# Two attention layers and a mixture of experts on one core: the program rewritten so that two heads share the array in 64-row tiles

## What is computed

```python
def attn_a(x):                       # 16 heads of 16 features
    q, k, v = x @ Wq.T + bq, x @ Wk.T + bk, x @ Wv.T + bv
    scores = q @ k.T / 4 - slope[h] * |pos_q - pos_k|     # -inf where pos_k > pos_q
    return softmax(scores) @ v @ Wo.T + bo
def attn_b(x):                       # K, Q, V = split(x @ W_KQV.T); rope on Q and K; causal
    return softmax(rope(Q) @ rope(K).T / 4) @ V @ W_O.T
def ffn(x):                          # 8 experts, two per token, chosen by expert_indices
    ys = gelu(xs @ w1[e]) @ w2[e]    # xs: token rows sorted by expert
    return sum over the two of ys * weight, for 1024 tokens, + bias
x = x + attn_a(layernorm(x)); x = x + ffn(layernorm(x))
x = x + attn_b(layernorm(x)); x = x + ffn(layernorm(x))
```

## Time and profile before

| what | value |
|---|---|
| median of three runs | 5482.74 us (5477.25 to 5489.55) |
| the profiled execution, first to last instruction | 5479.5 us |
| TensorE busy | 4942.7 us, 90% |
| VectorE busy | 3575.6 us, 65% |
| ScalarE busy | 3156.7 us, 58% |
| GpSimd busy | 584.8 us, 11% |
| granted TensorE clock, mean | 0.956 |

### The profile page before, as it was taken

One profiled execution on the slowest core, in us unless ns is written; L12 is line 12 of the kernel. 1 busy time (PEld: TensorE's weight loads), 2 busy tenths in 40 slices (PEclk: granted clock), 3 DMA queues, 4 the chain that ended last, 5 costly groups with the idle time before them and its releaser, 6 DMA issues.

```text
span 5479.5 us, 115362 instructions
## 1 busy us (share of the span) xinstructions
PE 4942.7 (90%) x29820; PEld 2236.2 (41%) x29820; DVE 3575.6 (65%) x9222; ACT 3156.7 (58%) x6661; POOL 584.8 (11%) x1479
## 2 busy tenths in 40 slices
PE   5999899998999899969689998999979998899897
PEld 2333433343333433358433334333433334333376
DVE  5778577857776677730377765778567785777600
ACT  2777566765666466732246772667536674566622
POOL 1000110011000200020210002000110002100101
PEclk9999999999999999989899998999989999999998
DMA  4221121103110311045221101211021111111154
GB/s 110 48 35 22 44 58 35 29 25 71 31 32 8 80 28 35 15 144 182 75 49 25 31 8 41 57 30 25 25 56 29 25 19 42 42 31 25 53 169 142
DMA packets 193432, 278.45 MB, mean 51 GB/s; under 512 B 45000, under 2 KB 155848, under 8 KB 192224
## 3 DMA queue, kind: packets, MB, share of 16 engines
q1 hardware_dynamic: 189664, 261.84, 20.4%
q0 software_dynamic: 3072, 8.39, 0.5%
HBM read 124.59 MB, written 43.25 MB: 31 GB/s over the span
## 4 chain that ended last, share of the span: by engine, by line
PE 73%; issue 11%; DVE 6%; ACT 5%; POOL 2%; DMA 1%; SPq 1%; ACTq 1%; DVEq 0%; another core or an unknown queue 0%; POOLq 0%
PE ps_acc L824 18%; PE ps_s L796 17%; PE ps_m L771 15%; ACT probs L597 3%; PE ps_s L931 3%; PE ps_s L748 3%; PE ps_o L834 3%; PE ps_s L799 2%; PE ps_m L941 2%; PE ps_o L941 2%; PE ps_s L910 2%; DVE ps_m L1048 2%; ACT acc_sb L590 2%; PE ps_acc L748 1%; DVE parts L1119 1%
## 5 line engine op out<-in xcount | busy, mean ns | idle before, releaser
L597 ACT ACTIVATE probs<-ps_s 128x512 f32<-128x512 f32 (+3 forms) x5120 | 2459.2, 538 | 1110.1 <-PE ps_s L796 641.7
L1051 DVE TENSOR_REDUCE part_max<-ps_m 128x1 f32<-128x512 f32 x3072 | 1998.2, 684 | 318.1 <-PE ps_m L771 317.1
L771 PE MATMUL ps_m<-stacks 108*128 108x512 bf16 (+7 forms) x5120 | 1790.0, 354 | 156.7 <-DVE part_max L1051 69.6
L796 PE MATMUL ps_s<-stacks 111*128 111x512 bf16 (+7 forms) x5120 | 1757.3, 356 | 98.5 <-issue 54.6
L1048 DVE CUSTOM_DVE_ANT_0 ps_m<-ps_m,mask 128x128 f32<-128x128 f32 (+3 forms) x2048 | 1002.8, 500 | 491.4 <-PE ps_m L771 482.0
L824 PE MATMUL ps_acc<-probs,v_head 128*32 128x512 f32 (+3 forms) x11264 | 1272.1, 516 | 1.9
L796 PEld LDWEIGHTS ps_s<-stacks 111*128 111x128 bf16 (+1 forms) x5120 | 498.7, 98 | 1362.9 <-ACT probs L597 997.1
L771 PEld LDWEIGHTS ps_m<-stacks 108*128 108x128 bf16 (+1 forms) x5120 | 503.3, 98 | 702.1 <-DVE part_max L1048 229.3
L799 PE MATMUL ps_s<-early,identb 128*128 128x128 bf16 x2048 | 453.7, 222 | 0.0
L824 PEld LDWEIGHTS ps_acc<-probs,v_head 128*32 128x32 f32 x11264 | 315.2, 108 | 333.1 <-issue 145.2
L504 POOL CAST cpart<-negmax 128x8 bf16<-128x8 f32 x256 | 50.8, 198 | 3315.2 <-DVE negmax L1056 3315.2
(11 more groups left out here) (114 smaller groups left out, 3362.7 us busy)
## 6 DMA issues: line engine op xcount, KB each, us to landing
stacks<-parts SPq DMA_DIRECT2D x1536, 64.0 KB
stacks<-w_dram SPq DMA_DIRECT2D x60, 1024.0 KB
stacks<-crow SPq DMA_DIRECT2D x768, 2.0 KB
xn<-x_in_dram SPq DMA_DIRECT2D x4, 2048.0 KB, 15.8
xb<-x_in_dram SPq DMA_DIRECT2D x4, 2048.0 KB, 8.4
x_before_ffn<-xb SPq DMA_DIRECT2D x8, 1024.0 KB, 5.2
x_after_a<-parts SPq DMA_DIRECT2D x4, 2048.0 KB, 10.7
xn<-x_after_a SPq DMA_DIRECT2D x4, 2048.0 KB, 15.0
```

Source lines behind the costliest of these rows:

```text
L597: act.activation(probs[:, n % 8, 0:QW - q0], ps_s[:, s_bank(j, n)[0], q0:QW], ACT.Exp)\
L771: pe.matmul(ps_m[:, bank, 0:w], q_stack(slot)[0:rows, qb * P:(qb + 1) * P], k_stack(slot)[0:rows, kc * QW:kc * QW + w], start=True, stop=T ...
L796: mm = pe.matmul(ps_s[:, bank, q0:QW], k_stack(slot)[0:rows, kb * P:(kb + 1) * P], q_stack(slot)[0:rows, qt * QW + q0:(qt + 1) * QW], star ...
L1051: dve.reduce_max(part_max[:, qb, kc:kc + 1], ps_m[:, bank, 0:w], AX_X).then_inc(item_used, 1)
```

## The change

The whole program is written anew. What it computes, the ffn's tiles and the order of layers and batches are the same. What differs:

- **Two heads at once.** A pair of heads has one q and one k stack, one head in rows 0 to 63 and the other in rows 64 to 127: 48 product rows (three products of two parts), 4 rows of positions, 2 of the maximum. The stacks are of type float32r instead of bf16. Scores (`score`, L817) and maxima (`unit`, L842) are issued as matmuls of 54 or 52 rows for head 0 and head 1 in turn, into different banks.
- **36 steps for 40 blocks.** On the diagonal the block 384 wide and the one 128 wide share a bank (`STEP`, `UNIT`), so that one exponential serves both. All masks are added by TensorE, 64 columns at a time (L825, L850), for the maxima too.
- **Maxima.** VectorE takes the maxima of both heads in one instruction over two banks (L1074), from two pairs of banks `ps_p`. It splits the maximum itself, in two parts.
- **Values.** Groups of two or three steps; the four 32-column tiles are now head 0 and 1 x outer and inner query blocks, 256 columns each (L874). They sum up in `ps_acc` by themselves: `sum_up` and `turn_sum` are gone. ScalarE copies 256 columns (L718) and SP stores them to DRAM in four transfers (`store_o`, L541).
- **Banks.** Scores of both heads and the five kinds of TensorE's job (`RING_JOBS`) take turns in one ring of three banks, `ps_r`.
- **Fronts and backs inside the heads.** `batch_jobs` cuts the next batch's front and the last batch's back into jobs (`ld`, `ln`, `xt`, `qk`, `v`, `sp`, `st`; `rl`, `bl`, `bm`, `y`, `ba`, `bs`) of one quarter batch or less, and hangs them on steps of the pairs. Those of TensorE stand two by two behind the values at seven of the 18 double steps (`JOB_STEPS`). The norm of 512 rows is cut in eight parts (`norm`), with Newton steps from an integer estimate instead of a square root on ScalarE. Q and k parts go to DRAM (`parts_d`) and come back per pair; rope swaps neighbours by transfer (`sw`) instead of by a second projection.
- **No loops.** All 64 pairs are written out. The first batch's front stands alone ahead of them, the last batch's back among the last ffn's tiles (`AFTER_AT`). The first ffn stops the pairs at the half; its gather and sum run within the next pair.

The core of the diff:

```diff
-BLOCK = [(qt, kb, max(0, P * (kb - 4 * qt))) for qt in reversed(range(NQ)) for kb in range(4 * qt + 4)]
...
+STEP = [slot for qt in reversed(range(NQ)) for slot in
+        [[(qt, kb, 0, 0)] for kb in range(4 * qt + 1)] +
+        [[(qt, 4 * qt + 1, P, 0), (qt, 4 * qt + 3, 3 * P, 3 * P)], [(qt, 4 * qt + 2, 2 * P, 0)]]]
...
+        while at:
+            n = 3 if len(at) == 3 else 2
+            groups.append(at[:n])
+            at = at[n:]
...
+JOB_STEPS = (2, 10, 16, 20, 24, 28, 34)
...
+            def score(g, n, heads):
...
+                for at, (qt, kb, q0, col) in enumerate(STEP[n]):
+                    for u in heads:
+                        if at == 0:
+                            pe.wait_ge(ring_used, PLACE[("s", g, n, u)] - RING + 1)
+                        r = slice(HALF * u, HALF * u + ROWS)
+                        mm[u] = pe.matmul(block_bank(g, n, u)[:, col:col + QW - q0], ks[s][r, kb * P:(kb + 1) * P],
+                                          qs[s][r, qt * QW + q0:(qt + 1) * QW], start=at == 0, stop=True,
+                                          skip_group_check=True)
+                for qt, kb, q0, col in STEP[n]:
+                    for part in range(2 if kb >= 4 * qt else 0):
+                        for u in heads:
+                            r = slice(HALF * u, HALF * u + HALF)
+                            lo = col + HALF * part
+                            mm[u] = pe.matmul(block_bank(g, n, u)[:, lo:lo + HALF], mk[r, 2 + part, :], id64[r, :],
+                                              start=False, stop=True, skip_group_check=True)
...
+            def unit(g, n):
...
+                if at >= 2:
+                    pe.wait_ge(p1_used, at - 1)
...
+            def times_v(g, grp):
...
+                        for u in range(2):
+                            for inner in range(2):
+                                chunks = [c for c in ((1, 2) if inner else (0, 3)) if c >= first]
...
+                                mm = pe.matmul(ps_acc[tile:tile + DH + 1, to[0] * P:(to[-1] + 1) * P],
+                                               v_head[:, beta % 2, kb, 2 * p + u, :], src, start=kb == 0,
+                                               stop=n == GROUP[LAST_GROUP[qt]][-1], skip_group_check=True)
...
-                pieces = [(r, r, BLOCK[4 * g + r][2], QW) for r in range(4)]
...
-            def sum_up(ly, hb, h):
...
+            def exp_block(g, n, u):
+                w, at = step_width(n), STEPS * g + n
+                if at >= PBUF:
+                    act.wait_ge(pv_mm, groups_to(at - PBUF))
+                act.wait_ge(s_mm[u], at + 1)
...
+                for qb, kc, w, col in UNIT[n]:
+                    mm = dve.tensor_reduce(part_max[:, :, qb, kc], ps_p[:, p1_banks(g, n), col:col + w], AX_X, ALU.max)
+                mm.then_inc(p1_used, 1)
```

More of the change, by code:

```diff
@@ new lines, with value_groups @@
+assert STEPS == len(UNIT) == 36
+HI_UNITS = sum(1 for slot in UNIT if slot[0][0] >= TT // 2)
+FIRST_LO = next(n for n, slot in enumerate(STEP) if slot[0][0] == 1)
+def value_groups():
+    groups = []
+    for qt in reversed(range(NQ)):
+        at = [n for n, slot in enumerate(STEP) if slot[0][0] == qt]
+        while at:
+            n = 3 if len(at) == 3 else 2
+            groups.append(at[:n])
+            at = at[n:]
+    return groups
+GROUP = value_groups()
+GROUPS = len(GROUP)
+GROUP_OF = {n: i for i, steps in enumerate(GROUP) for n in steps}
@@ new lines, with slots_from @@
+GROUP_AT = {2 * (steps[-1] // 2 + 1): i for i, steps in enumerate(GROUP)}
+assert len(GROUP_AT) == GROUPS and GROUP_AT[STEPS] == GROUPS - 1
+LAST_GROUP = {qt: max(i for i, steps in enumerate(GROUP) if STEP[steps[0]][0][0] == qt) for qt in range(NQ)}
+EVAC_STEP = {qt: 2 * (GROUP[i][-1] // 2 + 1) + 1 for qt, i in LAST_GROUP.items() if qt}
+LATE_EVAC = 1
+C_HI, C_LO = 30, 6
+JOB_STEPS = (2, 10, 16, 20, 24, 28, 34)
+assert all(n in GROUP_AT for n in JOB_STEPS + (C_HI, C_LO))
+def slots_from(t, n):
+    found = []
+    while len(found) < n:
+        if t % STEPS in JOB_STEPS:
+            found += [t, t]
+        t += 1
+    return found[:n]
@@ new lines, in store_o @@
+            def store_o(g, qt):
+                e = evac_index(g, qt)
+                beta, p = divmod(g, PAIRS)
+                sp.wait_ge(acc_out, e + 1)
+                for u in range(2):
+                    row = o_d[beta % 2, 2 * p + u, :, qt * QW:(qt + 1) * QW].rearrange("r (c n) -> r c n", n=P)
+                    for inner in range(2):
+                        to = row[:, 1:3, :] if inner else row[:, 0::3, :]
+                        tile = 32 * (2 * u + inner)
+                        src = acc_sb[tile:tile + DH + 1, e % 2, :].rearrange("p (c n) -> p c n", n=P)
+                        sp.dma_start(to, src).then_inc(o_st[e % 2], 16)
@@ L696, in _ @@
-                turn_slots(0, 0)
-                with act.Fori(0, ETILES // 2) as ip:
-                    for s in range(2):
-                        hidden(2 * ip + s, s, True)
-                hidden(ETILES - 1, 0, False)
+                        act.wait_ge(h_mm, at * NF + f + 1)
+                        if f == 0 and i:
+                            act.wait_ge(fy_mm, 2 * at)
+                        act.activation(hid[:, f, :], ps_p[:, f % 4, 0:ET], ACT.Gelu).then_inc(gelu_out, 1)
+                    if ly:
+                        for j in AFTER_AT.get(i, []):
+                            job(*j)
@@ L729, in project @@
-            def project(ly, b16, job):
-                kind, i = JOBS[job]
-                back = (4, 2)[ly]
-                if job >= back:
-                    pe.wait_ge(*freed(ly, b16, *JOBS[job - back]))
-                if kind == "v":
-                    to = ring(job * (1, 2)[ly])
+            pe.wait_ge(consts_in, CONSTS - 16 * 4)
+            pe.wait_ge(acc_clear, 1)
+            pe.matmul(ps_acc[:, :], zeros[:, :], mk[:, :, :].rearrange("p a n -> p (a n)"), start=True, stop=True)
@@ L738, in project @@
                                        start=(k == 0), stop=(k == KD - 1))
[L739 to L746 removed]
+                elif kind == "y":
@@ L960, in done @@
+            for j in BEFORE:
+                job(*j)
+            count = 0
             def done(ins):
@@ L1190 @@
+            for n in range(STEPS):
+                unit(0, n)
+            for g in range(NG):
+                for n in range(STEPS):
+                    if g + 1 < NG:
+                        unit(g + 1, n)
+                    for j in JOBS[g][n]:
+                        job(*j)
+                if g % (NG // 2) == NG // 2 - 1:
+                    experts(g // (NG // 2))
+            for k in range(TOPK):
+                mix(1, k)
 def kernel(**inputs):
```

1630 lines of the change are left out of this document (783 added, 847 removed).

## The result

The changed kernel takes **4413.9 us** (median of 4 runs, 4405.6 to 4420.2) against 5482.7 before: 0.8048 of the time, 95% interval 0.8033 to 0.8063. It lies inside the predicted range, 304 us above the forecast of 4110 and 54 above the forecast's own range.

A forecast was written before the change was run, and what follows sets the result against it. VectorE paces and jobs are not hidden: 54 us a pair. Start 166 + 63 x 54 + last pair 42 + ffns 222 and 275 = 4107, forecast 4110 us; own range 3900 to 4360, whole range 3680 to 5000.

The forecast's parts named there:

- VectorE paces, 42.1 us without norms: Ordinary double step of the pairs: VectorE needs 2.37 us, ScalarE 2.2, TensorE 1.96; 42.1 us a pair without norms.
- TensorE's 1.96 us a step: TensorE's need in an ordinary double step: 4 x 0.213 + 0.85 + 0.26 = 1.96 us.
- One cycle a column and two tiles beside each other: Scores and maxima in float32r: one cycle a column, two 64-row tiles side by side, 14.5 us for both heads.
- Rivals A and B: Tiles not overlapping, or two cycles, 4610 to 5370, 0.20; float32r at float32's four cycles a column, 6500, 0.08.
- Jobs in full: TensorE's front and back jobs in the pairs are not hidden: 0.87 us each, 65 a batch, 8 a pair.
- Rival C: Jobs in the pairs hidden after all: a pair 46 to 48 us, the whole 3640 to 3730, chance 0.10.
- Masks: 128 mask matmuls of 64 columns a pair, as 64 couples at 0.055 us: 3.5 us on TensorE.
- Exponentials at 0.552, maxima at 1.18: 512-wide exponentials every 0.552 us, ScalarE 43.5 a pair; two-bank maxima 1.18 us back to back, VectorE 45.1.
- the signs: VectorE, ScalarE near 80% busy, TensorE near 85; ScalarE's wait almost none without jobs; falls if pair off over 4 us.
- First ffn: First ffn: 209 us and 13 for its first weights, which wait for the probabilities' space, 222 in all.
- The 20 us for output jobs: Second ffn: 16 output jobs between its tiles, each waiting for its copy in one bank, 20 of 275 us.
- wanted one pair later: SP's in-order queue: a wait in `store_o` delays stack loads, but these are wanted one pair later.

The follow-up runs named there:

- four banks: Changed kernel with maxima left out from the second pair on and a ring of four banks instead of three: 3629.4 us, ratio 0.6646.
- the one other order tried here: Changed kernel with the values issued ahead of the second head's score of the second step: 4686.4 us, ratio 0.8547.

## Why the prediction was right, and where it was off

- **Direction and size.** Right in direction, and 4414 lies in the whole range of 3680 to 5000, which was made wide for rivals that did not come; it lies outside the forecast's own. The engine that was to pace did not, so that the size came so near owes something to luck. The terms, by the profile: start 163 against 166; 64 pairs 3670 (1833 to the first ffn, 1837 behind it) against 63 x 54 + 42 = 3444; first ffn 230 against 222; second with the end 342 against 275. Together 297 too little, 226 of it in the pairs.
- **The step that failed: "VectorE paces, 42.1 us without norms", an ordinary double step of 2.37.** It is 2.66 and VectorE is not awaited in it. I had compared what three engines need and taken the largest. What decides is a chain through two of them that a ring of three closes: 0.59 to land, 0.6 for one exponential, and 1.42 from the waiting score through the values to the next. In a pair without jobs the eleven double steps whose scores have no mask take 30.6 us (seven at 2.66, three at 2.88, one at 3.33) where 2.37 each would be 26.1; the seven others take 18.0 of the 19.9 that were left of the predicted 46. That is 48.6 against 46, 166 us over 64 pairs. The rest of the 226 are jobs, the last pair (51 against 42) and pairs at a granted clock of 0.76 to 0.97 just before and behind the ffns.
- **TensorE's 1.96 us a step.** Too low: 2.44, worked out from the rows above. Four couples were charged, but the waiting score runs alone and makes a fifth place; the first couple behind the values holds it for 0.34 and not 0.21, and 0.22 goes by at the switch to the values. The runs without maxima and with shorter exponentials show that this did not set the time.
- **One cycle a column and two tiles beside each other.** Right. The scores of both heads are one row of two (1026.43) and the next row is 0.23 or 0.34 later. Rivals A and B fell with it. Weight loads of the float32r stacks take 186 ns and are hidden except behind a switch: the scores and maxima of one head use the same rows of the array and follow each other at 0.23 with 0.213 of streaming. The Trainium skill (TensorE: Matmul & The Clock Gate, Part 3, The mechanism) has a load overlap a running matmul only where the row group differs; by that rule they would follow at 0.4, and the trace disagrees for 64-row tiles as it did for the full array.
- **Jobs in full.** Right: 68 us a batch against 65, and 0.96 for one of two in a double step against 0.87. Rival C fell; it fell even with four banks. (Its lower end, by the prediction's own sum, is 4107 - 63 x 8 = 3603 and not 3640.)
- **Masks.** Charged 3.5 us a pair, worth 1.2 to 1.8: most lie in waits. This error went the other way and hid some of the first.
- **Exponentials at 0.552, maxima at 1.18.** Exponentials run every 0.48 us when the bank is there ((2.06 - 0.60) / 3), so ScalarE's 43.5 us were too much; maxima at 1.18 right. Of the signs, VectorE and ScalarE near 80% busy and TensorE near 85 came out as 66, 63 and 94, and "without jobs almost none" of ScalarE's waiting as 0.60 us a double step: these spoke against the reading. A pair of 57.1 against 54 stayed within the 4 us that were set.
- **First ffn.** 8 us late: its tiles take 14.3 us and not 13.9, the first 16.6. From the last value matmul to the first of the hidden layer 13.2 us went by, as charged; 9.0 of them are the first weights' transfer. Behind it the first pair ran with a granted clock of 0.58 for 20 us, mostly the lower level, 1.2 GHz (window 2225 to 2245), and took 79.7 us, 26 more than the first pair of another batch.
- **Second ffn.** The 20 us for output jobs left out what SP's queue does beside them: four rows of the chain with 9.7 to 10.7 us of waiting for the next tile's rows. That what SP brings is "wanted one pair later" held for the pairs and not there.

## What to carry to other kernels

Before dividing work by engine, write down the loops: for each ring of buffers, from one use to the use that waits for it, with the latencies and with everything that the waiting instruction has queued behind it. Such a loop can pace a kernel in which every engine has slack. Then a faster engine helps only by what of it stands in the loop (nothing for VectorE, one exponential of four for ScalarE), and the one other order tried here made it slower; another buffer, or a shorter member of the loop, does help. And test a bound by taking the suspected work away: the maxima were nearly all that VectorE did and half of TensorE's short matmuls, and leaving them out changed the step at full clock by nothing.

## What the runs showed of the hardware

- Leaving out work made a kernel slower: without maxima the granted clock fell from 0.970 to 0.888 and the time rose by 156 us, with a pair at full clock 0.9 us shorter. Faster values gave 0.838, and there the same kind of pair took 41.0 us at a granted clock of 1.00 and 55.4 at 0.50. What a change takes from TensorE it may pay back in clock.
- Two extra matmuls in 14 of 18 double steps raised the clock by 0.06 and four by 0.08.
- Matmuls in float32r stream about one column a cycle (512 columns every 0.23 us, where 512 / 2400 is 0.213) with a weight load of 186 ns, against 98 for bfloat16 in the earlier trace rows.
- A store of 128 KB took 1.7 us with nothing issued just ahead of it and 8.9 behind two transfers of 1 MB and one of 256 KB from the same queue.
